# One block for the first stage and the attention, with the routing spread over its first two steps

## What is computed

```python
xn = _layernorm(x)
out = x + attn_block(xn) + moe_ffn(xn)
# attn_block(xn): h = xn + attention(LN(xn)) @ out_U @ out_V + out_b
#                 h + gelu(LN(h) @ fc1_U @ fc1_V + fc1_b) @ fc2_U @ fc2_V + fc2_b
# attention: 16 heads of 8, causal in sequences of 256, q/k/v as x @ U[h] @ V[h] + b
# moe_ffn(xn): top 2 of 9 experts by softmax(xn @ Wr), hidden size 352, silu(gate) * up
```

## Time and profile before

| | us |
|---|---|
| median of 3 runs (1087.9 to 1090.06) | 1088.07 |
| the profiled execution's own time | 1088.45 |
| its span in the trace | 1086.7 |
| TensorE busy in it | 998.2 |
| VectorE busy in it | 713.5 |
| mean clock granted to TensorE | 0.936 of full |

### The profile page before, as it was taken

The page is one execution under the profiler, slowest core; times in us unless marked ns, Lnnn a source line. Parts: engine busy times, 40 slices in busy tenths (PEclk is TensorE's granted clock), DMA queues, the critical chain, the costliest instruction groups (busy, mean ns, idle before and its releaser), DMA issues. The chain is left out here.

```text
span 1086.7 us, 25509 instructions
## 1 busy us (share of the span) xinstructions
PE 998.2 (92%) x7780; PEld 795.0 (73%) x7812; DVE 713.5 (66%) x3239; ACT 564.2 (52%) x1285; POOL 387.7 (36%) x509
## 2 busy tenths in 40 slices
PE   0697479999999999999999996999999999999997
PEld 0696255666666666666666664999999999999886
DVE  6254566777777777777777784455555555458887
ACT  0372025655565655565565566555555555564442
POOL 1003542434433434443434432354444544441010
PEclk9655659999999999999999999899999999999999
DMA  8569542444444444544544421422222222218784
GB/s 245 185 225 363 138 81 70 109 111 96 114 108 111 118 103 97 121 104 103 121 107 93 98 61 36 120 62 62 72 64 61 62 74 63 80 41 257 223 226 135
DMA packets 146754, 128.17 MB, mean 118 GB/s; under 512 B 18560, under 2 KB 128512, under 8 KB 146624
## 3 DMA queue, kind: packets, MB, share of 16 engines
q1 hardware_dynamic: 117344, 72.45, 24.7%
q0 software_dynamic: 17808, 47.35, 16.4%
q10 hardware_dynamic: 11472, 6.75, 2.3%
HBM read 57.68 MB, written 43.13 MB: 93 GB/s over the span
## 5 line engine op out<-in xcount | busy, mean ns | idle before, releaser
L1200 DVE CUSTOM_DVE_ANT_0 att_masked_st<-att_m_ps,att_mask_st 128x128 bf16<-128x128 f32 (+1 forms) x1024 | 312.2, 354 | 109.1 <-PE att_m_ps L915 70.1
L1105 ACT ACTIVATE att_probs<-att_t_ps 128x512 f32<-128x512 f32 x384 | 229.2, 598 | 190.7 <-PE att_t_ps L939 141.3
L833 POOL DMA_INDIRECT slot_x<-att_xs,att_slot_now x128 | 128.1, 1001 | 265.8 <-PE att_t_ps L939 166.1
L1431 POOL DMA_INDIRECT y_scratch<-moe_y,moe_row_now x136 | 131.1, 964 | 153.6 <-issue 82.7
L1679 DVE TENSOR_TENSOR moe_hidden<-moe_gate,moe_up_ps 128x352 f32<-128x352 f32 x136 | 70.9, 521 | 111.1 <-issue 82.1
L1508 PE MATMUL moe_y_ps<-w_down,moe_hidden_t 128*128 (+1 forms) x816 | 114.0, 276 | 1.4 <-issue 1.1
L1606 ACT ACTIVATE moe_gate<-moe_gate_ps 128x352 f32<-128x352 f32 x136 | 63.0, 463 | 94.6 <-PE moe_up_ps L1491 94.6
L939 PE MATMUL att_t_ps<-att_mask_ts,att_ident_b 128*128 128x256 bf16 (+1 forms) x352 | 111.3, 316 | 0.0
L1508 PEld LDWEIGHTS moe_y_ps<-w_down,moe_hidden_t 128*128 128x128 f32 (+1 forms) x816 | 101.8, 191 | 3.1 <-issue 3.0
L1200 DVE DVE_READ_ACCUMULATOR2_ANT att_row_max<- 128x1 f32 x1024 | 85.3, 83 | 0.2
L938 PE MATMUL att_t_ps<-even_stack,att_k_stack 97*128 97x512 f32 x192 | 81.3, 424 | 3.4 <-DMA even_stack<-att_neg_max 3.3
(11 more groups left out here) (257 smaller groups left out, 2170.2 us busy)
## 6 DMA issues: line engine op xcount, KB each, us to landing
slot_x<-prep_blank POOLq DMA_DIRECT2D x17, 516.0 KB, 12.9
moe_x<-slot_x SPq DMA_DIRECT2D x34, 258.0 KB
att_xs<-xn_scratch SPq DMA_DIRECT2D x32, 256.0 KB
att_k_stack<-att_k_hi POOLq DMA_DIRECT2D x64, 128.0 KB
mlp_rows<-y_scratch POOLq DMA_DIRECT2D x16, 512.0 KB, 5.5
xn_scratch<-prep_xn SPq DMA_DIRECT2D x16, 256.0 KB, 2.6
xt_scratch<-prep_xt SPq DMA_DIRECT2D x16, 256.0 KB, 2.1
att_xt<-xt_scratch SPq DMA_DIRECT2D x16, 256.0 KB, 2.9
```

Source lines behind the costliest of these rows:

```text
L833: pool.indirect_dma_start(env["slot_x"][:], bass.IndirectOffsetOnAxis(ap=slot_now[c.parity][:, col:col + 1], axis=0), xs[c.parity][:, t, k ...
L1105: act.activation(probs[:, m % PT, :], t_ps[m % 2][:], ACT.Exp).then_inc(exp_done, 1)
L1200: last = dve.tensor_tensor_reduce(out=masked_st[m % 2][:, part], in0=m_ps[m % 2][:, part], in1=mask_st[:, SEQ - width:], scale=1.0, scalar ...
L1431: pool.indirect_dma_start(env["y_dram"][:], bass.IndirectOffsetOnAxis(ap=row_now[q.parity][:, t:t + 1], axis=0), y[c.parity][:], None).the ...
```

## The change

`prepare` and `attention` become one function, `first_and_attention`, with one block. Line numbers here are those of the new kernel.

- The first stage's arrays lie in memory that the attention uses later. x and the routing arrays lie in `first_words`, which is the place of the expert weights `w_gate_up` and `w_down`; xn, the scaled xn and the turned chunk (`xn_made`, `xnr`, `xt_made`) lie in `att_probs`; q's and k's parts lie in `att_qk_parts`.
- So the expert weights can't be loaded at the start. SyncE loads one expert, in five transfers, in each of the steps 3 to 11, after the second stack of q and ahead of the copy of the maxima.
- All products of weights and the biases are made ahead of the loop. The vectors and small matrices are loaded by SyncE behind x; ScalarE issues the U and V loads once the first quarter of x has landed.
- The router's scores are made with the router's weights as the stationary operand, into four groups of 32 columns (L873), copied by ScalarE, and turned back (L879).
- The projections of chunks 0 and 1, their stacks, and the first seven units of maxima stand inside the loop. Eight of the 17 blank fills move from the loop into step 0, and the scatter of a chunk comes one step later.
- The routing is cut into links. Four stand behind the loop among the last units of maxima, 29 in the slots of step 0 and three in step 1; its matmuls stand in slots 4, 7 and 9 of step 0.
- ScalarE makes all four tiles of the scaled xn in each chunk, as it did before.

```diff
-        prepare(nc, locals())
-        attention(nc, locals())
+        first_and_attention(nc, locals())
...
+                def load_expert(e):
+                    sp.dma_start(w_gate_up[:, e, 0:FF].bitcast(F32), w["Wg"][e]).then_inc(experts_loaded, 16)
+                    sp.dma_start(w_gate_up[:, e, FF:2 * FF].bitcast(F32), w["Wu"][e]).then_inc(experts_loaded, 16)
+                    for c, (at_row, rows) in enumerate(FF_CHUNKS):
+                        sp.dma_start(w_down[0:rows, e, c, :], w["Wd"][e, at_row:at_row + rows, :]).then_inc(experts_loaded, 16)
...
+                    if W_FROM <= p.index < W_FROM + EXPERTS:
+                        if p.index == W_FROM:
+                            sp.wait_ge(routed_all, 1)
+                        load_expert(p.index - W_FROM)
...
+                for c in range(chunks):
+                    if c >= 2:
+                        store_xt(c)
+                    if c + 2 < chunks:
+                        store_xn(c + 2)
+                    if c == V_AT - 1:
+                        sp.wait_ge(cleared, 1)
+                        stack_q(at(0, 0), 0)
+                    if c == V_AT:
+                        stack_q(at(0, 0), 1)
...
+                    if c == Q_AT[1] + 3:
+                        sp.wait_ge(other_cleared, 1)
+                        stack_q(at(0, 1), 0)
...
+                def score(c):
+
+                    pe.wait_ge(xt_ready, c + 1)
+                    if c >= 2:
+                        pe.wait_ge(logits_copied, c - 1)
+                    for t in range(TPC):
+                        last = pe.matmul(score_ps[c % 2][32 * t:32 * t + 32, 0:P], w_router, xt_of(c)[:, t * P:(t + 1) * P], start=True, stop=True,
+                                         skip_group_check=True)
+                    last.then_inc(routed_t, 1)
...
+                EARLY_LINKS = {m: 1 for m in range(UNITS, EARLY)}
+                LINKS = ({0: 2, 1: 2, 2: 2, 3: 2, 5: 1, 6: 1, 7: 1, 8: 2, 9: 2, 10: 1, 11: 1, 12: 1, 13: 1, 14: 1, 15: 1, 16: 1, 17: 1, 18: 1, 19: 1, 20: 1,
+                          21: 1, 22: 1, 23: 1}, {3: 1, 5: 1, 7: 1})
...
+                        if x < 2:
+                            for _ in range(LINKS[x].get(slot, 0)):
+                                next(routing)
```

## The result

The changed kernel takes 1086.2 us (median of 20 runs, 1078.1 to 1099.1), the kernel before 1088.9 in as many: a ratio of 0.9967, 95% interval 0.9952 to 0.9982. So it is 0.3% faster, where 1.1% was forecast. The runs of the changed kernel scatter over 21 us, those of before over 5. The ratio leaves out three of its runs that were over 1.5% above its fastest.

A forecast was written before the change was run, and what follows sets the result against it. From step 2 on TensorE was taken as the bound, busy 31.96 of 32.1 us a step; the change works on the earlier stretches. Sum: 1088.45 − 28.8 + 11.0 + 5.4 = 1076 us, range 1058 to 1090.

The forecast's parts named there:

- (a): Everything up to the chunk loop: no net change, 0 us, with the loop's first transposition at 50 to 54 us.
- (b): From the loop's first transposition to step 0: 76.5 us against 105.3, −28.8, including 17 us of stalls from SyncE's blocks.
- rival B: In the chunk loop SyncE's blocks of stack transfers hide, so 17 us come back: 1059 us; chance 0.14.
- 512 columns at half clock: Projections in chunks 3 and 4 of the loop: 512 columns cost TensorE twice 0.40 us.
- Rival K: TensorE's clock rises in the loop; units of maxima and step 0's first slots gain about 5 us: 1071; chance 0.06.
- (c): Step 0: the routing work moved into its slots lengthens it by 11.0 us.
- with VectorE near full: Sign expected in step 0: it lasts 44 to 50 us with VectorE busy nearly throughout.
- rival C: Step 0 gives the gain back: TensorE gets gaps, its clock stays low, +10 us, so 1086; chance 0.14.
- What is late next is the first scores of step 1, nothing else: End of step 0: its lateness reaches only step 1's first scores; no further cost counted, 0 us for step 1.
- (d): Expert weights loaded ahead of the copy of the maxima: 0.6 us in each of 9 steps, +5.4 us.
- rival D: Slower: weights in front hold up the maxima in full, 2.2 to 2.6 us a step, 1091 to 1094; chance 0.16.
- (e): The rest, with blank fills moved to step 0 and the scatter one step later, on GpSimd: 0 us.

The follow-up runs named there:

- the wide counts: The changed kernel with the nine counting products of step 0's slot 4 moving 32 columns of ones each instead of one; one run, 1076.0 us.

## Why the prediction was wrong

The sign and the outer range held; the size did not, and the likeliest value was 10 us too low. By the spans the sum missed by 9.2 us: −1.4 in (a), −6.4 in (b), +1.6 in step 0, +5.6 in step 1, +7.9 in steps 2 to 14, and +2.0 behind. The first two hid part of the rest.

- **(a)** 1.4 us better than the 0 forecast: the first transposition of the loop is at 49.8 us, against 51.2, just outside the 50 to 54 that were named as the sign.
- **(b)** right in its mechanism, too small in size: from that transposition to step 0 there are 70.1 us where the sum has 76.5, so −35.2 for −28.8. The stalls behind SyncE's blocks came as worked out (gaps of TensorE of 9.7, 1.8, 5.0 and 1.3 us, 17.8 together, for the 17 of the sum, and spreading the blocks gives 12.6 back), so rival B is out. The miss lies in two terms. The lead-in and chunks 0 to 4 took 13.8 us (to the transposition at 63.6 us) for 17.0: there "512 columns at half clock" and the 1.09 us of turning took 0.50, and the clock was at the upper level from about 53 us on, with a turning at 0.66. (A projection of q is two such products: 1.02 us there and 1.91 at the lower level, not the 0.8 of the sum.) Chunks 5 to 7 took 18.5 (to 82.1 us) for 21.2, the second gap being short. The remaining parts are within 1.5 us of the sum. Rival K had a chance of 0.06; it came true only up to the first stall, and the units of maxima and step 0's first slots, where it saw its gain, ran at 0.50. With the old scoring step 0 starts 7.4 us later; that is the price of the old form and of the clock together, not of the clock alone.
- **(c)** near in size, +12.6 for +11.0, but by luck: the parts miss both ways. By TensorE's starts of slots, slots 0 to 11 took 32.6 us for 18.8 before, +13.8 where the sum has 3.6 + 5, and slots 12 to 23 took 16.9 for 18.1, −1.2 where it has +2.4. (It also took slots 0 to 3 of before as 6.6 us; the trace has 7.1.) VectorE's busy time grew by 12.4 us, not 16, and the sign "with VectorE near full" did not come: it is busy 35.0 of 49.4 us. In the middle of the step the limit is TensorE at half clock, 16 us of it, with 7.7 us of counting products from 130.7 to 149.5. That is rival C's mechanism over a third of the step. At full clock these 16 us would be 8, so the fall costs at most 8 us, an estimate. Taking the routing out of the steps removes links, products and most of the low clock together, so the runs don't divide the 12.6 among them; and why the clock fell stays open.
- **The step that failed first** is the sentence "What is late next is the first scores of step 1, nothing else", and with it the count of links that "the three in step 1" would cost nothing. VectorE left step 0 late, with the link of 1224 numbers still to do, and step 1 lost 5.6 us. Moving that link gave 3.8 back, 2.4 of them the clock's; with no links at all the step is 32.0.
- **The step that failed most** is (d), "So 0.4. Together 0.6 × 9 steps = 5.4". It measured 11.8 in the profiled execution, and 8.5 on the average of the profiled kernels. One load ahead of the maxima was taken as the price of five. The prediction's own sign of failure came with it: steps 5, 6, 9 and 10 passed 34 us. The mechanism is rival D's, the landing and not the issue (1.2 us or somewhat more), but it struck four of nine steps, with waits of 2.5, 1.2, 3.1 and 0.7 us; in the steps behind the two long waits the clock falls as well, to 0.95 over steps 6 and 10. D's 2.2 to 2.6 in every step was wrong too.
- **(e)** missed 2.0 us behind the start of step 15. TensorE waits 7.4 us for the first rows of the experts instead of 5.6, but in six of the other profiled kernels, with the same late scatter, it waits 5.5 to 5.7, so the later scatter is not shown to be the cause. This stretch varied from 443.7 to 450.4 us over the profiled kernels, in some with a wait of ScalarE whose releaser the trace doesn't name, so its cause stays open. (The sign "steps 13 and 14 at 32.1" was misread from the start: step 14 lasted 30.3 us before and 30.4 now.)

Open as well is why the weights strike just the four steps 5, 6, 9 and 10. An instruction transfer on q8 falls at the end of each of them and not in the other five; with the weights away the same steps wait 0.9 us or nothing. The other profiled kernels with the weights whole in front show the same four steps with waits, of 0.25 to 2.54 us. But in them a q8 transfer falls at the end of step 3 as well, mostly without a wait. So it is a coincidence shown in the traces, not tested, and q8 alone is not enough.

## What to carry to other kernels

A small transfer that a full engine waits for should have nothing large ahead of it, even where the queue has time to issue: look for an earlier gap of that queue in the step, here 11 us earlier and nearly free. A block of transfers in a queue that also stores from double buffers costs its length less the buffers' cover, so spread it. Work put into the gaps of an engine comes out late at the end of the stretch; carry the lateness into the next one before calling it hidden, and where it saves ahead of the stretch, price both sides: here 29.5 us saved for 19.0 paid. A sum that comes out near the measured time is checked part by part: here step 0 was near by two misses of opposite sign.

## What the runs showed of the hardware

- VectorE's product of 1224 numbers on one partition took 3.01 us beside GpSimd's addition, and 1.42 without it; GpSimd's small copy behind took 1.41 instead of 0.20. One and the other ran in turn, not side by side. The Trainium skill ("SBUF — State Buffer", "SBUF: two separate sides") says that the two engines lock a shared pair of ports for a whole instruction; these rows agree.
- Three loads of 127, 127 and 95 partitions held SyncE's queue for 23 us, those of 128, 128 and 96 for 1.4.
- TensorE was granted 0.84 and 1.00 of its clock in a loop in which it was busy 14.6 of the 20 us from 50 to 70, and 0.50 from 50 to 60 us, busy all the time, with the old scoring. The two kernels differ in the form of the scoring alone (narrow stationary operand, a copy, and a turning back).
- A fall of the clock is not tied to the kernel alone. Behind the same wait of 2.2 us in step 1 the clock over the step was 0.91 in the changed kernel and 1.00 with the wide counts, and in step 0 TensorE ran 16 us at 0.50 while busy all the time.
